# Filler work beside causal attention: one filler step per key tile in place of two, and the low-rank FFN's matmuls in steps of nine in place of four and five

## The reference

```python
x = x + _L0_attn_ref(_layernorm(x, axis=-1), Wqkv, bqkv, Wproj, bproj)
x = x + _L0_ffn_ref(_layernorm(x, axis=-1), W, b, V_r, C)
# attention: 16 heads of 64, softmax(q k^T / 8) with a causal mask, then out @ Wproj + bproj
# ffn: x @ W^T + b + (x @ V_r) @ C^T, V_r and C of rank 32
```

## Time and profile before

| what | value |
|---|---|
| median of 2 runs | 959.82 us (954.76 and 964.88) |
| the profiled execution, its own time | 961.39 us |
| its span, first to last instruction, slowest core (core 2) | 959.8 us |
| spans of the eight cores | 942.5 to 959.8 us |
| mean granted TensorE clock, by core | 0.827 to 0.851 |

### The profile page before, as it was taken

One profiled execution on the slowest core, in us unless ns is written; L12 is line 12 of the kernel. 1 busy time (PEld: TensorE's weight loads), 2 busy tenths in 40 slices (PEclk: granted clock), 3 DMA queues, 4 the chain that ended last, 5 costly groups with the idle time before them and its releaser, 6 DMA issues.

```text
span 959.8 us, 11446 instructions; the slowest of 8 cores (942.5 to 959.8 us)
## 1 busy us (share of the span) xinstructions
PE 733.8 (76%) x3433; PEld 300.2 (31%) x3433; DVE 280.2 (29%) x675; ACT 353.8 (37%) x769; POOL 185.5 (19%) x304
## 2 busy tenths in 40 slices
PE   0599999990688888788878787877788887865656
PEld 0244444440343333322223322322222332222222
DVE  2534343110253232432222232313111231143332
ACT  0131322220244553534454554655655365500000
POOL 2000000001253232422222222222201222022211
PEclk9999999996555575985888898989995687978797
DMA  8980100009400000110101010101010010101001
GB/s 172 216 170 23 66 22 1 1 1 159 104 1 1 1 24 0 44 45 1 45 1 44 1 44 1 44 1 45 1 44 1 8 37 1 44 23 66 23 22 44
DMA packets 15131, 38.18 MB, mean 40 GB/s; under 512 B 3401, under 2 KB 3425, under 8 KB 15073
## 3 DMA queue, kind: packets, MB, share of 16 engines
q0 software_dynamic: 7616, 11.67, 7.8%
q1 hardware_dynamic: 7457, 25.79, 7.5%
HBM read 39.68 MB, written 8.39 MB: 50 GB/s over the span
## 4 chain that ended last, share of the span: by engine, by line
PE 68%; DVE 12%; ACT 7%; issue 6%; DMA 3%; POOL 2%; DVEq 0%; SPq 0%; ACTq 0%; POOLq 0%
PE ps_pv L412 17%; PE ps_sp L428 7%; PE ps_w L544 6%; PE ps_sp L255 6%; PE ps_pv L255 6%; PE ps_w L615 5%; PE ps_u L428 4%; ACT xnt_a L435 4%; PE ps_pv L615 3%; PE ps_bf L239 3%; PE ps_sp L282 3%; PE ps_w L282 3%; ACT xf_a L435 3%; DVE wq_a L490 2%; DMA xf_a<-wffn 2%
## 5 line engine op out<-in xcount | busy, mean ns | idle before, releaser
L435 ACT ACTIVATE xnt_a<-ps_sp 128x512 bf16<-128x512 f32 (+3 forms) x285 | 142.6, 537 | 180.0 <-PE ps_sp L428 124.0
L428 PE MATMUL ps_sp<-q_fm,k_fm 64*128 64x512 bf16 (+3 forms) x427 | 136.8, 415 | 44.0 <-ACT xnt_a L435 28.3
L412 PE MATMUL ps_pv<-xnt_a,v_on 128*66 128x512 bf16 (+3 forms) x356 | 116.8, 435 | 2.1 <-POOL xnt_a L442 1.5
L442 POOL TENSOR_TENSOR xnt_a<-xnt_a,tri_sb 128x128 bf16<-128x128 bf16 x142 | 57.2, 425 | 290.6 <-ACT xnt_a L435 289.6
L428 PE MATMUL ps_u<-q_fm,k_fm 64*128 64x512 bf16 (+2 forms) x213 | 87.1, 409 | 25.9 <-ACT xf_a L435 17.0
L435 ACT ACTIVATE xf_a<-ps_u 128x512 bf16<-128x512 f32 (+3 forms) x142 | 75.9, 535 | 61.8 <-PE ps_sp L428 55.9
L412 PE MATMUL ps_pv<-xf_a,v_on 128*66 128x512 bf16 (+3 forms) x284 | 95.8, 438 | 1.7 <-POOL xf_a L442 1.3
L435 ACT ACTIVATE xf_a<-ps_sp 128x512 bf16<-128x512 f32 (+3 forms) x142 | 70.8, 539 | 64.1 <-PE ps_sp L428 43.5
L482 DVE RECIPROCAL recips<-ps_bf 128x4 f32<-128x4 bf16 x64 | 11.6, 182 | 252.0 <-PE ps_bf L472 248.7
L442 POOL TENSOR_TENSOR xf_a<-xf_a,tri_sb 128x128 bf16<-128x128 bf16 x114 | 46.2, 425 | 179.1 <-ACT xf_a L435 177.8
L428 PEld LDWEIGHTS ps_sp<-q_fm,k_fm 64*128 64x128 bf16 x427 | 31.1, 96 | 136.6 <-issue 133.1
(11 more groups left out here) (73 smaller groups left out, 737.5 us busy)
## 6 DMA issues: line engine op xcount, KB each, us to landing
xf_a<-x SPq DMA_DIRECT2D x32, 512.0 KB, 3.3
y<-xf_a SPq DMA_DIRECT2D x16, 512.0 KB, 2.7
wq_a<-wqkv POOLq DMA_DIRECT2D x3, 2048.0 KB, 38.4
wq_a<-wproj POOLq DMA_DIRECT2D x1, 2048.0 KB, 18.2
xf_a<-wffn POOLq DMA_DIRECT2D x4, 512.0 KB, 23.5
bias_a<-bqkv POOLq DMA_DIRECT2D x1, 512.0 KB, 55.6
bias_a<-bffn POOLq DMA_DIRECT2D x1, 512.0 KB, 59.5
bias_a<-bproj SPq DMA_DIRECT2D x1, 512.0 KB, 7.8
```

What stands on the lines that cost most here:

```text
L412: e.matmul(ps_pv[hd][0:66, off * 128:512], v_on[:, ki2, 66 * hh:66 * hh + 66], chunk(cb)[:, 0:ncol], start=st, stop=sp),
L428: e.matmul(sbanks[sb][:, off * 128:512], k_fm[hp:hp + 64, hc, ki * 128:(ki + 1) * 128], q_fm[hp:hp + 64, hc, g * 512 + off * 128:(g + 1) * ...
L435: e.activation(chunk(cb)[:, 0:ncol], sbanks[sb][:, off * 128:512], AF.Exp, bias=0.0, scale=0.125),
L442: gate = P.op("pool", lambda e, cb=cb: e.tensor_tensor(chunk(cb)[:, 0:128], chunk(cb)[:, 0:128], tri01[:], ALU.mult), waits=[m_ex, m_cm], ...
```

## The change

Two edits. `emit_B_pair` calls `pump()` once per ki in place of twice. In `gen_C2` the yield in the middle of each half goes, so that c has 7 yields in place of 9, and the eight matmuls of a half and the one with C are emitted in one step. `gen_C1a2` keeps its yields. No instruction is added, removed or given another operand; what changes is where in each engine's list the filler instructions stand.

```diff
@@ -448,7 +448,6 @@
                 if ki % 2 == 1:
                     pop_pv()
                 pump()
-                pump()
             pop_pv(drain=True)
             if defer is not None:
                 defer[1]()
@@ -618,8 +617,6 @@
                                   start=(kc == 0), stop=False),
                          waits=w0 if kc == 0 else [],
                          sig=None)
-                    if kc == 3:
-                        yield
                 mmf = P.op("pe", lambda e, half=half:
                            e.matmul(fdst(half), u_bf,
                                     ct_bf[0:32, half * 512:(half + 1) * 512],
```

## The result

The changed kernel takes 916.16 us (median of 11 runs) where the kernel before takes 964.74 (median of 10); the ratio is 0.952, with an interval of 0.949 to 0.956, so 4.8% faster. The forecast was 935 with a range of 910 to 963: the direction and the range hold, the gain is 1.7 to 1.9 times the 26 us that were forecast. The 1.9 has another base in it: with ten runs the kernel before has its median at 964.74, with two it had 959.82; the spans of the two profiled executions, 959.8 and 914.5, differ by 45 us.

What follows compares the result with a forecast made beforehand. No engine was full: TensorE waited on VectorE's answers, starving ScalarE, and ran partly at 1.2 GHz. The terms -33 - 3 - 12 + 7 + 15 = -26 us against 961.4 gave 935 us, range 910 to 963.

Steps and rivals of the forecast that it cites:

- Part A: Heavy pairs (c and a2 pumped in): TensorE's four waits on VectorE's answers mostly go, -33 us.
- Part B: Ten heavy pairs: filler work moves under ScalarE's pace, -3 us, between 0 and -10.
- Part C: Start of the eight last heavy pairs: half of the low-clock loss goes, -12 us, bounds 0 and -25.
- Part D: Pairs (2,0), (1,7), (1,6): new waits where work of 8-key-tile pairs laps over, +7 us, between 2 and 12.
- Part E: Four light pairs (b and a1) of 12 key tiles: ScalarE's Ln waits 3.85 us each for late statistics, +15 us.
- rival 3: Heavy and light pairs: clock improves throughout, -25 us at heavy pairs' starts, another -7 in light ones; 915 us, chance 0.12.
- The first: Light pairs of 12 key tiles: ScalarE stalls on Ln pull the clock down; 955 us, chance 0.22.
- The second: Heavy pairs: spread filler no longer brings the clock back, so slower; 990 us with five such pairs, chance 0.08.

Runs made afterwards that it cites:

- run with empty steps: Kernel before, two pumps and steps of four and five kept, six empty steps added in c where the pair has 12 or 16 key tiles: 936.04 us, 0.969.
- one pump alone: Kernel before with one pump per key tile only, the yields in c's halves kept (second edit left out): 893.66 us, 0.925.
- nines alone: Kernel before with steps of nine matmuls only, two pumps per key tile kept (first edit left out): 952.13 us, 0.987.

## Why the prediction was right, and where it was off

*Part A, the waits that go.* Right in place and size: 28.9 us in the eight last heavy pairs were to become 1.6, and 1.9 are left. In the two heavy pairs of g = 1, for which I gave 5.8 us, core 2 has 6.8 before (1.1 + 3.1 + 1.3 + 1.3), and core 3 has 0.7 of them after. The run with empty steps, with less spreading than the change, has most of the heavy pairs' gain.

*Part B, work under ScalarE's pace.* Small, as forecast: between the changed kernel and the run with empty steps lie 7 us in seven heavy pairs. But I did not ask the question for each edit by itself. The rule that I used, blocks of max(2.5, 1.7 + filler), says that nines hide worse than fours, and one pump alone has room for 14 steps at K = 16; one pump only would have come out ahead.

*Part C, the clock at the front of heavy pairs.* Mechanism right, size too small, and this is the term that was mis-sized. The eight last heavy pairs fell from 28.1 + 83.4 + 130.8 = 242.3 us to 22.5 + 63.8 + 107.4 = 193.7, by 48.6. Less 27.0 of waits and some 3 of B, 18 to 19 us are left for the clock, where I took 12. This is a remainder, but the granted clock agrees with it: by each pair's length and mean clock, the eight spent 60.3 us at the lower level before and 23.5 after (means of the cores). If TensorE paces the pair in such a stretch, half of these 36.8 us is lost, 18.4; that is an estimate. So the half that I let go should have been three quarters of the 25, and the heavy pairs came out shorter than the 27 to 29 and 22 to 24 us that I named as signs: 26.8 to 26.9 (K = 16) and, from (2,3) on, 20.7 to 21.9 on core 3 (K = 12).

*Part D.* +7 forecast. (2,0) took 6.8 us more and (1,6) 1.9, while (1,7) gained 2.0 net of its new wait. The three waits are 2.34, 1.85 and 4.46 against 1.5, 1.7 and 4.2.

*Part E.* +15 forecast; 17.2 by the pairs, 15.4 when the statistics alone were moved. The rule of the Trainium skill, "TensorE: Matmul & The Clock Gate", section "Architectural detail: the array is 16× 32×32, not 1× 128×128", that ScalarE's and VectorE's queues are strictly first in, first out, agrees with the trace: no exp passed the Ln that idled ScalarE for 3.81 us.

*What was not in the sum.* The light pairs of 16 key tiles gained 7.4 us (73.8 to 66.4) because (3,4) and (3,6) no longer stay at the low clock. I had this as rival 3 with 7 us and a chance of 0.12, and priced nothing of it in the forecast. The pairs up to (1,3) gained 4.0, which I gave as unchanged; the second profile of the kernel before has 98.7 there and not 100.8, so about half of it is scatter. The base moved by 5 us between two runs and ten.

The sum by pairs: -48.6 in the eight heavy pairs, +17.2 in the light ones of 12, -7.4 in those of 16, and -4.0 up to (1,3). For (1,4) to (2,0) it is 88.5 against 89.4: -7.5 in (1,5), -2.0 in (1,7), +1.9 in (1,6), +6.8 in (2,0), nothing in (1,4). Together 43.7 us, and the mean span of the eight cores fell from 953.1 to 909.9.

*The rivals.* The first, that the stalls of E pull the clock down for a whole light pair, did not come: on core 3 the four are at 0.84 to 0.87, so they come back within the pair. The second, slower, did not come; heavy pairs of g = 2 and 3 have a clock of 0.86 to 1.00 on that core. (Its sum was a pair off: -14 + 9 x 2 is above zero already.) What the Trainium skill, "TensorE: Matmul & The Clock Gate", section "Loop structure matters more than you think", says of long waits between bursts, that they lose the clock, is borne out in its direction by the heavy pairs, whose waits were short ones: four of 0.5 to 1.55 us went and the clock rose. That denser bursts as such keep it is not: nines alone left the heavy pairs as they were. The third rival gave 915 us, next to the 916.16 measured, with a chance of 0.12. Its mechanism came in part: the light pairs' 7 us did (7.4), and of C's 25 us 18 to 19; the rest of the nearness is the pairs up to (1,3) and the base, which it did not speak of, and so luck.

*Still open.* Why a light pair, attention alone, stays at the low clock from end to end in one order of work and comes back in another. It did so in the kernel before and in the run with empty steps, each with two pumps, and never in (3,2) to (3,6) with one pump; but nines with two pumps had it in (2,2) and not there. No run here takes this apart.

## What to carry to other kernels

In this schedule, which is only an order of emission, the distance from an answer to its user was worth more than how far the work was spread: put a step of the other stream between them. Look then at what each engine's own queue puts ahead of a short instruction on which another engine waits: three small statistics behind twelve other instructions cost 3.8 us each time here, and moving them by one line gave 1.5%. And when a change has two edits, work out each alone and on top of the other: of these two, the first gained 7.5% alone, the second 1.3% alone, and on top of the first the second gave back 2.5%.

## What the runs showed of the hardware that was not expected

TensorE can be busy for 86% of a stretch and stay at the low clock: (3,4) of the kernel before is busy for 25.09 of 29.1 us at 0.54. But for eight transposes of 128 by 128 early in the pair (and the eight of `normalize`), its matmuls have 64 rows or 66 columns; whether that matters no run tells. In one order of work this happened in the same pair on five and six of eight cores in two executions, and reordering filler in other pairs made it go or move. For such a stretch the price is 7 us in 29, against 21.7 us for the same pair at 0.92 in the changed kernel.
